# Cross-attention stack on one core: part of the second layer's subtractions and all epsilons on GpSimd, layer norm ends and value and key diagonals on ScalarE

## The reference

```
layer 1 (l0): x = x + tanh(gate) * attn16(x, ln(ctx)*g + b)             16 heads of 16
layer 2 (l1): x = ln(x + attn32(x, ctx, 8 key/value heads) Wo + bo) * gamma + beta    eps 1e-6
layer 3 (l2): h = x + attn16(ln(x)*g1+b1, ctx); x = h + gelu(ln(h)*g2+b2 ...) MLP, eps 1e-5
layer 4 (l3): two attentions with 16 heads of 128 and an added bias key, then an MLP
```

## Time and profile before

| | |
|---|---|
| median of 3 runs | 1161.63 us (1161.3 to 1162.51) |
| profiled execution | 1164.01 us, span 1162.0 us |
| TensorE matmul | 1057.9 us busy, 91% of the span |
| VectorE | 689.0 us, 59% |
| ScalarE | 442.5 us, 38% |
| GpSimd | 390.3 us, 34% |
| mean granted TensorE clock | 0.976 of full speed |

### The profile page before, as it was taken

How to read it: one execution, slowest core, us unless ns; L and a number is a source line. 1 busy time by engine, 2 the same in 40 slices (tenths; PEclk the granted TensorE clock), 3 DMA queues, 4 the chain that set the end, 5 groups by cost and what they waited for, 6 DMA issues and landing times.

```text
span 1162.0 us, 16862 instructions
## 1 busy us (share of the span) xinstructions
PE 1057.9 (91%) x6772; PEld 814.7 (70%) x6772; DVE 689.0 (59%) x1191; ACT 442.5 (38%) x829; POOL 390.3 (34%) x346
## 2 busy tenths in 40 slices
PE   6999887777789889998999999999999999978998
PEld 4667454444567678887777777777787777657997
DVE  4656999789987532572444544675454454563552
ACT  2555444344446422223423333332333332323543
POOL 2546667655776421220111111332112111222230
PEclk9999999888999999999999999999999999998999
DMA  9000000000000080000000012220000000100000
GB/s 312 30 2 1 1 1 1 1 1 1 1 1 2 1 307 1 1 1 1 1 2 1 1 37 95 94 66 1 1 1 1 1 1 4 71 0 1 28 20 28
DMA packets 17186, 32.47 MB, mean 28 GB/s; under 512 B 3538, under 2 KB 8404, under 8 KB 16596
## 3 DMA queue, kind: packets, MB, share of 16 engines
q1 hardware_dynamic: 17108, 31.39, 7.8%
HBM read 29.29 MB, written 2.10 MB: 27 GB/s over the span
## 4 chain that ended last, share of the span: by engine, by line
PE 74%; DVE 12%; ACT 5%; POOL 5%; issue 4%; DMA 0%; POOLq 0%; DVEq 0%
PE work L671 10%; PE work L783 10%; PE scores L722 9%; PE work L739 5%; PE scores L635 5%; PE work L648 5%; PE work L772 4%; PE work L509 3%; DVE smax L956 3%; PE work L551 3%; PE scores L500 2%; PE work L473 2%; POOL pair L1563 2%; PE work L754 2%; PE work L396 2%
## 5 line engine op out<-in xcount | busy, mean ns | idle before, releaser
L1530 POOL TENSOR_TENSOR stat<-stat,minus_half 128x2 f32<-128x2 f32 (+1 forms) x49 | 38.1, 778 | 327.9 <-DVE stat L892 327.9
L783 PE MATMUL work<-pair,probsT 128*128 128x256 f32 x512 | 123.6, 396 | 11.0 <-ACT pair L1449 8.8
L783 PEld LDWEIGHTS work<-pair,probsT 128*128 128x128 f32 x512 | 98.0, 196 | 36.3 <-issue 20.3
L671 PE MATMUL work<-ctxT,w 128*128 128x128 f32 x1024 | 120.2, 275 | 3.5 <-ACT pair L1440 1.6
L671 PEld LDWEIGHTS work<-ctxT,w 128*128 128x128 f32 x1024 | 118.2, 192 | 5.2 <-issue 3.1
L722 PE MATMUL scores<-pair,act_bufs 128*128 128x512 f32 x256 | 115.2, 592 | 0.0
L1440 ACT ACTIVATE pair<-work 128x512 f32<-128x512 f32 x64 | 38.2, 598 | 154.3 <-PE work L739 154.3
L1638 POOL TENSOR_TENSOR probs<-probs,smax 128x1024 f32<-128x1024 f32 x22 | 42.0, 1907 | 160.5 <-DVE smax L1202 160.5
L1430 ACT ACTIVATE kvT<-work,cols 128x128 f32<-128x128 f32 x128 | 36.6, 369 | 154.5 <-PE work L671 154.5
L1182 DVE TENSOR_REDUCE smax<-scores 128x16 f32<-128x1024 f32 x32 | 39.2, 1225 | 76.9 <-PE scores L722 76.9
L722 PEld LDWEIGHTS scores<-pair,act_bufs 128*128 128x128 f32 x256 | 46.4, 190 | 46.0 <-issue 45.9
(11 more groups left out here) (157 smaller groups left out, 2363.3 us busy)
## 6 DMA issues: line engine op xcount, KB each, us to landing
w<-in_l_wk SPq DMA_DIRECT2D x8, 512.0 KB, 6.2
w<-in_l_wq SPq DMA_DIRECT2D x8, 512.0 KB, 6.8
w<-in_l_wv SPq DMA_DIRECT2D x8, 512.0 KB, 7.0
w<-in_l_wo SPq DMA_DIRECT2D x8, 512.0 KB, 8.0
out<-x SPq DMA_DIRECT2D x8, 256.0 KB, 2.1
x<-in_x SPq DMA_DIRECT2D x1, 1536.0 KB, 9.2
pair<-in_l_fc SPq DMA_DIRECT2D x1, 1024.0 KB, 7.2
pair<-in_l_pr SPq DMA_DIRECT2D x1, 1024.0 KB, 10.8
```

The lines of the kernel that those rows point to most:

```text
L671: last = mm(bank[:, h * P:(h + 1) * P], w[:, c, (4 * g + h) * K3:(4 * g + h + 1) * K3], ctxT[:, c, p * P:(p + 1) * P], start=(c == 0), sto ...
L783: last = mm(step_banks(j + 1)[0][:, 0:D], probsT_bufs[j % 2][:, q, :], pv[n % 2][:, bb, q, :], start=(q == 0), stop=(q == GH // 2 - 1))
```

## The change

Units, tiles, buffers and arithmetic stay. What moves:

- In the second layer the maximum of the tiles 1 and 3 is subtracted by GpSimd (`tile_shifted` there, semaphore `p_sub`), that of 0 and 2 still by VectorE. In GpSimd's order tile 1's subtraction stands ahead of gamma and beta, tile 3's ahead of the sums of tile 2.
- Every epsilon is added by GpSimd, just ahead of its power (`rstd`).
- The norm ends of "l1" and "l2" are ScalarE activations, `x * rstd + (-mean * rstd)`; VectorE computes the small product (`ln_shift`).
- The value diagonals are two ScalarE activations per unit with a 0/1 scale per row. For the second layer GpSimd clears each of the three buffers once. The key diagonals of the second layer are eight ScalarE activations; those of the other layers stay on GpSimd.
- The masks `pair16` and `pair8` and their DMAs go; a small mask `half` comes.

```diff
@@ tensor: waits (queries, reciprocals_transposed and weighted: d_vd becomes a_vd)
-                e.wait_ge(p_kd, u + 1)
+                if layer == 1:
+                    e.wait_ge(a_kd, b + 1)
+                else:
+                    e.wait_ge(p_kd, b + 1 if layer == 0 else B + b + 1)
@@ vector: ln_stats loses
-                v.tensor_scalar(per_tile[:, :, 8], per_tile[:, :, 7], eps, None, ALU.add).then_inc(d_var, 1)
+            def ln_shift(what):
+                st = stat[LN[what] % 4][:, 0:12 * TT].rearrange("p (t k) -> p t k", k=12)
+                e.wait_ge(p_rstd, LN[what] + 1)
+                v.scalar_tensor_tensor(out=st[:, :, 10], in0=st[:, :, 6], scalar=-1.0, in1=st[:, :, 9], op0=ALU.mult,
+                                       op1=ALU.mult).then_inc(d_shift, 1)
@@ vector: unit_values (all of it) goes
@@ vector: tile_max, tile_shifted
+                if layer == 1 and t == 1 and k >= FIRST[B] + 2:
+                    e.wait_ge(p_sub, (k - FIRST[B]) // 2)
...
-                    v.tensor_tensor(e3, e3, bmax, ALU.subtract).then_inc(d_sub, 1)
+                    if t == 0:
+                        e.wait_ge(d_max, k + 1)
+                        v.tensor_tensor(e3, e3, bmax, ALU.subtract).then_inc(d_sub, 1)
@@ vector: loop over the units
-                if u + 1 < NU:
-                    unit_values(u + 1)
                 if tiles:
                     tile_shifted(*tiles[0])
                 if ended[0] == 1:
-                    ln_finish(("l1", ended[1]), xb(ended[1]), xb(ended[1]), TT)
+                    ln_shift(("l1", ended[1]))
...
-                    ln_finish(("l2", b), xb(b), norm[b % 3], TT)
+                    ln_shift(("l2", coming[1]))
@@ scalar: new functions
+            def unit_values(u):
...
+                for h in range(2):
...
+                    last = act(dst, src, ACT.Copy, scale=half_of_row[:, 16 * h:16 * h + 1])
+                last.then_inc(a_vd, 1)
+            def key_diagonal(u):
...
+                for i in range(8):
+                    last = act(kd[:, :, i, :], kT_small[1][:, :, b * S:(b + 1) * S], ACT.Copy,
+                               scale=head_of_row[8][:, i:i + 1])
+                last.then_inc(a_kd, 1)
+            def ln_finish(what, src, dst):
+                st = stat[LN[what] % 4]
+                e.wait_ge(d_shift, NORMS[what][1])
+                for t in range(TT):
+                    last = act(dst[:, t, :], src[:, t, :], ACT.Identity, bias=st[:, 12 * t + 10:12 * t + 11],
+                               scale=st[:, 12 * t + 9:12 * t + 10])
+                last.then_inc(a_norm, 1)
@@ scalar: exponentials
-                    e.wait_ge(d_sub, k - FIRST[B] + 1)
+                    e.wait_ge(d_sub if k % 2 == 0 else p_sub, (k - FIRST[B]) // 2 + 1)
@@ scalar: loop over the units
                 if u + 2 < NU:
                     unit_source(u + 2)
+                if u + 1 < NU:
+                    unit_values(u + 1)
                 if u > 0:
                     probs_out(FIRST[u] - 1)
                 if tiles:
                     exponentials(tiles[0][0])
                 if u > 0:
                     reciprocals_out(u - 1)
+                if ended[0] == 1:
+                    ln_finish(("l1", ended[1]), xb(ended[1]), xb(ended[1]))
                 if tiles:
                     probs_out(tiles[0][0])
                     exponentials(tiles[1][0])
+                if u + 2 < NU and UNITS[u + 2][0] == 1:
+                    key_diagonal(u + 2)
+                if coming[0] == 2:
+                    b = coming[1]
+                    if b >= 3:
+                        e.wait_ge(pe_x, 2 * B + b - 2)
+                    ln_finish(("l2", b), xb(b), norm[b % 3])
@@ gpsimd: rstd
-                e.wait_ge(d_var, LN[what] + 1)
+                e.wait_ge(d_agg, AGGREGATES[what])
+                g.tensor_scalar(per_tile[:, :, 8], per_tile[:, :, 7], 1e-6 if what[0] == "l1" else 1e-5, None,
+                                ALU.add).then_inc(p_var, 1)
+                e.wait_ge(p_var, LN[what] + 1)
@@ gpsimd: new function
+            def tile_shifted(k):
+                e3 = probs[k % 4][:, 0:GS].rearrange("p (h s) -> p h s", s=S)
+                e.wait_ge(d_max, k + 1)
+                g.tensor_tensor(e3, e3, smax[k % 2][:, 0:GH].unsqueeze(2).broadcast_to([P, GH, S]),
+                                ALU.subtract).then_inc(p_sub, 1)
@@ gpsimd: loop over the units
-                if u + 2 < NU:
+                if u + 2 < NU and UNITS[u + 2][0] != 1:
                     key_diagonal(u + 2)
+                if u + 1 < NU and UNITS[u + 1] in ((1, 0), (1, 1), (1, 2)):
+                    e.wait_ge(pe_av, group_of(FIRST[u - 1]))
+                    g.memset(vdiag[(u + 1) % 3], 0.0).then_inc(p_zero, 1)
...
                 if tiles:
                     tile_sums(tiles[0][0])
+                if len(tiles) == 4:
+                    tile_shifted(tiles[1][0])
                 if ended[0] == 1:
...
                 if coming[0] == 2:
                     rstd(("l2", coming[1]), TT)
-                for tile in tiles[1:-1]:
-                    tile_sums(tile[0])
+                if len(tiles) == 4:
+                    tile_sums(tiles[1][0])
+                    tile_shifted(tiles[3][0])
+                    tile_sums(tiles[2][0])
```

More of the change, by code:

```diff
@@ L235, in flat @@
             return v.rearrange("p a b -> p (a b)")
-        names = ["ctx", "ident", "cols", "head16", "head8", "pair16", "pair8", "mask", "x0", "x1", "rows_early", "rows_late",
+        names = ["ctx", "ident", "cols", "head16", "head8", "half", "mask", "x0", "x1", "rows_early", "rows_late",
                  "mask_tok", "l2_fc", "l2_pr", "l3_fc", "l3_pr"]
@@ L270, in build @@
         p_xb, p_mul, p_l1, p_xm, p_xl, p_pr = (sem(f"p_{n}") for n in ("xb", "mul", "l1", "xm", "xl", "pr"))
-        p_wg = sem("p_wg")
+        p_wg, p_zero, p_sub, p_var = (sem(f"p_{n}") for n in ("wg", "zero", "sub", "var"))
         order = ["ctx"]
@@ L283, in build @@
         LN = {what: i for i, what in enumerate(order)}
+        AGGREGATES, NORMS, on_act, on_dve = {}, {}, 0, 0
+        for what in order:
+            AGGREGATES[what] = max(AGGREGATES.values(), default=0) + (CN if what == "ctx" else TT)
+            if what[0] in ("l1", "l2"):
+                on_act += 1
+                NORMS[what] = (a_norm, on_act)
+            else:
+                on_dve += 1
+                NORMS[what] = (d_norm, on_dve)
         STEPS = range(-4, 4 * 2 * PAIRS + 1)
@@ L879, in vector, with ln_stats @@
             bn = agg = 0
-            def ln_stats(what, src, eps, tiles):
+            def ln_stats(what, src, tiles):
                 nonlocal bn, agg
                 st = stat[LN[what] % 4]
+                before = order[LN[what] - 4] if LN[what] >= 4 else None
+                if before in NORMS and NORMS[before][0] is a_norm:
+                    e.wait_ge(*NORMS[before])
                 for t in range(tiles):
@@ L1334, in unit_keys @@
                     act(dst, bank[:, :], ACT.Identity, bias=col(bk, o)).then_inc(a_key, 1)
+            def unit_values(u):
+                layer, b = UNITS[u]
+                hd, vd = LAYERS[layer]["hd"], vdiag[u % 3]
+                e.wait_ge(pe_v, u + 1)
+                e.wait_ge(s_in["half"], 16)
+                if u >= 3:
+                    e.wait_ge(pe_av, group_of(FIRST[u - 2]))
+                if layer == 1 and b < 3:
+                    e.wait_ge(p_zero, b + 1)
+                for h in range(2):
+                    if layer == 1:
+                        src = work[3][:, 0:D].rearrange("p (q e h m) -> p q e h m", e=2, h=2, m=8)[:, :, :, h, :]
+                        dst = flat(vd).rearrange("p (q r m) -> p q r m", r=8, m=8)[:, :, h:8:6, :]
+                    else:
+                        src = work[3][:, 0:D].rearrange("p (q h m) -> p q h m", h=2, m=hd)[:, :, h, :]
+                        dst = vd[:, 0:8, h * hd:(h + 1) * hd]
+                    last = act(dst, src, ACT.Copy, scale=half_of_row[:, 16 * h:16 * h + 1])
+                last.then_inc(a_vd, 1)
+            def key_diagonal(u):
+                layer, b = UNITS[u]
+                kd = kdiag[u % 4].rearrange("p (c i s) -> p c i s", c=DC, s=S)
+                e.wait_ge(a_key, 2 * layer + 2)
+                e.wait_ge(s_in["head8"], 16)
+                e.wait_ge(pe_sc, FIRST[u - 3])
+                for i in range(8):
[9 more added lines that the diff above has]
+                last.then_inc(a_norm, 1)
             def exponentials(k):
@@ L1372, in scalar @@
                 tiles = tiles_of(u) if u < NU else []
+                ended = UNITS[u - 2] if u >= 2 else (0, 0)
+                coming = UNITS[u + 3] if u + 3 < NU else (0, 0)
                 if u + 2 < NU:
                     unit_source(u + 2)
+                if u + 1 < NU:
+                    unit_values(u + 1)
                 if u > 0:
```

84 lines of the change are left out of this document (31 added, 53 removed).

## The result

The changed kernel takes 1186.43 us (median of 4 runs, 1184.99 to 1188.17) against 1162.07 (4 runs, 1161.3 to 1163.76): ratio 1.0208, 95% interval 1.0188 to 1.0228, 24 us slower. Its profiled execution took 1187.42 us, span 1185.2. The forecast was 1177, with a range of 1166 to 1187.

The account below looks back on a forecast made before the run. The prediction took one chain VectorE-ScalarE-GpSimd to bound the second-layer units. Its terms summed to +15.5 us on the profiled 1164.01, so 1179.5, and 1177 after taking 2.4 off for the median; range 1166 to 1187.

Parts of the forecast that it names:

- The chain, not VectorE's fullness: Second-layer units: one chain VectorE-ScalarE-GpSimd sets the time, not one full engine; unit 11 goes to 24.1 us, +1.3.
- "some 2" and "some 4": Units 10 and 11: us that VectorE would idle before the sum of tile 1 and before that of tile 2.
- The collision: Unit 11: VectorE's subtraction of tile 2 goes in after GpSimd's multiply and holds back its add, +1.0 us.
- Key diagonal ahead of the queries: ScalarE, units 6 and 7: eight activations delay the queries, 1.05 us before unit 7, 0.95 before unit 8; +2.0 together.
- Units 8 to 11 and 13 to 15: Second layer: unit 8 +1.5 us, 9 +0.8, 10 and 11 +2.6 together; 13 to 15 +0.5, +2.3, +2.8.
- Unit 12: The third layer's keys wait for VectorE's residual, so their start and all behind it come 2.7 us later.
- Units 16 to 18: No GpSimd subtraction, shorter norm on VectorE, but queries behind the norm on ScalarE: -0.8 us in all.
- Epsilons: On GpSimd 0.5 us more each: +0.5 at the kernel's start, +0.4 at the third layer's first MLP norm.
- Rival 3: Units 8 to 15: VectorE is the bound and GpSimd's work lies beneath it; faster, 1148 us, 1134 at best; chance 0.11.
- rival 2: TensorE at half clock after idling delays second scores in units 9 to 11, partly 14, 15: +8, 1185 us; chance 0.15.
- Rival 1: Same chain, but collisions miss in units 10 to 12, epsilons and activations cost little: +10.5, 1172 us; chance 0.14.
- rival 4: Whole kernel: the moves cancel, VectorE's relief against the chain's growth; within 0.2%, 1162 us; chance 0.04.

Follow-up runs that it names:

- sums_later: Changed kernel with VectorE's sum of tile 1 put behind mask and maximum of tile 3: 1176.90 us, ratio 1.0117 to the kernel before.
- subs_only: Kernel before with only the subtractions of tiles 1 and 3 moved to GpSimd: 1189.78 us, ratio 1.0229 to the kernel before.
- subs_back: Changed kernel with all four subtractions of a second-layer unit on VectorE again: 1165.14 us, ratio 1.0020 to the kernel before.
- queries_first: Changed kernel with the third layer's norm end put behind the queries on ScalarE: 1181.38 us, ratio 1.0159 to the kernel before.
- key_after_queries: Changed kernel with the key diagonal on ScalarE moved behind the next unit's queries and tile 2's copies: 1186.31 us, ratio 1.0204 to the kernel before.
- shift_later: Changed kernel with the coming norm's product L910 put behind VectorE's subtraction of tile 2 in units 13 to 15: 1179.29 us, ratio 1.0158.
- no_sub_key_first: Changed kernel with all four subtractions on VectorE and norm ends, gamma and beta, later sums and key diagonals reordered: 1144.30 us, ratio 0.9845 to the kernel before.

## Why the prediction was right, and what was mis-sized

- **The chain, not VectorE's fullness.** Right. The unit's times from its zero, by the walk and measured: GpSimd's first subtraction over at 9.65, measured 9.8; multiply and add over at 12.25, measured 12.35; tile 1's sum over at 14.6 plus the collision's 1.0, measured 15.8; second subtraction over at 19.0 plus 1.0, measured 20.2; unit 24.1, measured 24.49. VectorE's idle times, "some 2" and "some 4", are 1.98 and 4.06, and it is busy 16.94. The subtractions' price, 1.90 from the fourth layer, holds to the digit. sums_later confirms the cause by removing it. One sign came out otherwise: units 8 to 15 were to take 206 to 208 us and took 210.0.
- **The collision** had the right price and another victim. VectorE's subtraction of tile 2 came at 11.8 of the unit (tile 2's scores were 0.90 late), not at 10.7, so it was held by the add (1.67 for 1.22) and then held GpSimd's add for tile 1 (2.27 for 1.27).
- **Key diagonal ahead of the queries.** Forecast 1.05 in unit 7 and 0.95 in 8; the run that takes it away gives back 1.11 and 1.11. Eight activations take 2.44 (forecast 2.3), 0.305 apiece. The lateness of 1.3 before unit 8 doesn't follow from the working as written, since 2.3 less a slack of 0.8 is 1.5; the trace has 1.27.
- **Units 8 to 11 and 13 to 15.** Forecast 5.85 for the first four, key diagonal included, measured 7.4; forecast 5.6 for the last three, measured 7.3. The missing 1.7, under 0.6 a unit, is less than the product L910, to which I gave no length and which took 1.22 to 1.25 in each beside GpSimd's add; about 0.7 a unit was won back elsewhere, and where stays open. Moving the product gave 2.1 in each unit (its length and the wait that it puts on VectorE; the split was not measured).
- **Unit 12**: the keys' start 3.0 us later, as the forecast 2.7 had it (23.4 of the unit against 20.4), but the eight matmuls took 1.4 less, so +1.57. That this term came out 1.1 under its forecast is the clock's scatter, and so luck.
- **Units 16 to 18 is the mis-sized term: -0.8 forecast, +5.9 measured**, an error of 6.7 in the 7.7 us by which the growth of the profiled span, 23.2, exceeded the sum, 15.5. I had seen that "queries now [stand] behind the norm on ScalarE" and took the norm to be ready in time. It is not: the power stands on GpSimd behind multiply and add, L910 waits for it and is stretched, and only then do norm and queries run. subs_only, without the ScalarE norm ends, has 38.06 us in these units (38.01 before), subs_back has 43.02, and queries_first 36.82. So the queue position is what the term had wrong: taking it away gives back 7.1 us, and without it the -0.8 would have been -1.2. How much it costs depends on the clock, for key_after_queries and shift_later have the norm end in the same place and 41.4 and 41.5 us in these units.
- **Epsilons.** I took 0.5 more than on VectorE. The operation takes 0.23, and from the aggregate's start to the power's it is 0.70 (341.61 to 342.31 in the changed kernel) against 0.58 in subs_only (188.66 to 189.24): 0.12 more. The start moved by +1.2, but it lies between 33.81 and 35.06 in kernels that are the same there, 34.84 in subs_only with the epsilon on VectorE: the term can't be told from that scatter. After the last unit nothing was lost (-1.2 for the forecast +0.4).
- **The rivals.** Rival 3 (VectorE the bound) is refuted by the waits of 1.98 and 4.06. Of rival 2 (clock) the condition came true, PEclk is 0.85 in unit 11 for 0.97; its price there did not: the second tile's scores end 4.7 after the zero, and VectorE starts on them at 4.8 without a wait. A smaller price came one tile later: from 187.67 to 192.30 the granted clock is 0.52, three groups of matmuls there (L405, L449, L521) take 2.0 us more than at the full clock (1.11 for 0.66, 1.98 for 1.08, 1.78 for 1.09), and VectorE waits 0.90 for tile 2's scores. Whether that 0.90 lengthened the unit was not tested. Rival 1 (the collisions miss) fell with the add of 2.27, rival 4 (the moves cancel) with the time.

The result lies 9.4 us above the forecast and only 0.6 below the range's upper end. The larger part of that is one term with the wrong sign; that it stayed inside owes something to luck, since unit 12 and the end of the kernel came 2.8 us under their terms for reasons that the prediction did not have.

Why do the repaired versions win? In no_sub_key_first the value and key diagonals and the norm ends are off VectorE and GpSimd, and every queue has the work that someone waits for first: VectorE is busy 19.25 of 20.74 in unit 11, waits for GpSimd 0.29 and 0.71, and TensorE's clock is 1.00 there. So these moves and these orders together are worth 1.6%, and what hid it was the subtractions (6.5 us for one of them alone, in the best order found), two places in ScalarE's queue, and two orders on VectorE and GpSimd that the change left as they were. The kernel before with these two orders alone was not run, and the diagonals and the norm ends were not tried one by one, so how much of the 1.6% each gives by itself stays open.

## What to carry to other kernels

When work moves to another engine, walk that engine's whole queue past the place where it is put: ask what stands behind it and who waits for that, as the norm end ahead of the queries cost 7.1 us here (queries_first) while the engine itself was busy 8.05 of 15.09 in unit 17. A full engine is relieved only by work that the receiving engine can do before it is needed; two subtractions of 1.22 us on VectorE became 1.90 us each on an engine that was already in the chain. And split a change with several moves: its halves stood at +2.3% and +0.2%, and the second of them, with orders to match, at -1.6%.

## What the runs showed of the hardware

- A VectorE operation on 2 columns of a small buffer (L910) takes 0.15 us undisturbed (193.27 in unit 11 of the changed kernel) and 1.22 when it starts 0.07 after a GpSimd add of 1.27; beside GpSimd's copies, 0.74 for two, it took 0.36 (178.25 in no_sub_key_first). What is left of the neighbour counts, not its own length. The Trainium skill, "SBUF — State Buffer", section "Who interferes with whom", says that a VectorE instruction with two SBUF inputs contends with a GpSimd instruction that reads SBUF, and that the shared ports are an exclusive lock; these rows agree, 1.22 us being the add's length less the 0.07 (1.20).
- Activations of 128 columns, SBUF to SBUF with a scale per row, cost 0.305 us apiece in a row of eight (2.44 us at 114.71 in the changed kernel).
- A GpSimd tensor_scalar on 2 columns takes 0.23 us (228 ns mean over 48 in the changed kernel), a third of the power's 0.73.
- The same eight matmuls (L413 or L422 in unit 12), behind stand-stills of 7.05 to 7.11 us, took 5.29, 6.30, 6.63 and 6.73 us; behind 3.06 us 3.70 in one kernel and 5.40 in another, behind 3.11 us 6.72. What decides how soon the clock is back stays open; the length of the idle time alone does not decide it.
